# Last layer: POOL takes the subtractions that split queries and keys into bf16 parts

## The reference

```python
def _L3_attn_ref(x, Wq, Wk, Wv, Wo):      # N_HEADS 16, head width 8, sequence 256
    q = shape_heads(x @ Wq.T)
    k = shape_heads(x @ Wk.T)
    v = shape_heads(x @ Wv.T)
    q = q * cos + _rotate_every_two(q) * sin
    k = k * cos + _rotate_every_two(k) * sin
    scores = jnp.einsum('bhqd,bhkd->bhqk', q, k) * scale
    scores = scores + mask[None, None]
    attn = jax.nn.softmax(scores.astype(jnp.float32), axis=-1).astype(q.dtype)
    out = jnp.einsum('bhqk,bhkd->bhqd', attn, v)
    ...
    return out @ Wo.T
```

## Time and profile before

| | |
|---|---|
| time, median of 3 runs | 768.75 us (766.16 to 769.16) |
| profiled execution, its own time | 766.3 us |
| span of the profiled execution | 765.0 us |
| busy: PE, PEld, DVE, ACT, POOL | 720.3, 572.4, 499.3, 441.5, 252.3 us |
| mean granted TensorE clock, share of full speed | 0.972 |

### The profile page before, as it was taken

The page is one execution under the profiler, slowest core; times in us unless marked ns, Lnnn a source line. Parts: engine busy times, 40 slices in busy tenths (PEclk is TensorE's granted clock), DMA queues, the critical chain, the costliest instruction groups (busy, mean ns, idle before and its releaser), DMA issues.

```text
span 765.0 us, 14977 instructions
## 1 busy us (share of the span) xinstructions
PE 720.3 (94%) x5760; PEld 572.4 (75%) x5760; DVE 499.3 (65%) x1321; ACT 441.5 (58%) x944; POOL 252.3 (33%) x267
## 2 busy tenths in 40 slices
PE   7799999999999889999999999999979799999996
PEld 4577886678787667877779998698768467767764
DVE  1656788548967766668763757476548477776652
ACT  4526788458885785686635655235421465554664
POOL 1375355562515722233670126851003500000000
PEclk8869999999999999999999999999999899999999
DMA  9811453425311140000026664568885404207000
GB/s 298 251 54 45 138 163 95 138 84 165 88 50 46 34 153 1 1 1 2 29 86 202 200 191 146 185 197 253 261 219 125 90 16 117 58 2 160 17 17 15
DMA packets 71221, 84.00 MB, mean 110 GB/s; under 512 B 7199, under 2 KB 55914, under 8 KB 71146
## 3 DMA queue, kind: packets, MB, share of 16 engines
q1 hardware_dynamic: 67054, 74.65, 33.7%
q0 software_dynamic: 4096, 8.40, 3.6%
HBM read 65.46 MB, written 17.43 MB: 108 GB/s over the span
## 4 chain that ended last, share of the span: by engine, by line
PE 77%; DVE 6%; DMA 5%; ACT 5%; POOL 4%; issue 2%; SPq 1%; POOLq 0%; ACTq 0%; DVEq 0%
PE bank L929 5%; PE bank L938 4%; PE bank L861 4%; PE bank L849 3%; PE bank L674 3%; PE bank L536 3%; PE bank L495 3%; PE bank L720 3%; PE bank L496 2%; PE bank L697 2%; PE bank L807 2%; PE bank L893 2%; PE bank L789 2%; PE bank L590 2%; PE bank L666 2%
## 5 line engine op out<-in xcount | busy, mean ns | idle before, releaser
L1970 DVE TENSOR_REDUCE arena<-bank 128x2 f32<-128x512 f32 (+1 forms) x96 | 63.7, 684 | 20.7 <-PE bank L763 11.1
L1285 ACT ACTIVATE arena<-bank 128x512 f32<-128x512 f32 x96 | 55.9, 597 | 35.7 <-PE bank L791 27.8
L495 PE MATMUL bank<-ones 128*128 128x256 bf16 x275 | 69.1, 282 | 2.9 <-POOL ones L2277 1.7
L496 PE MATMUL bank<-ones 128*128 128x256 bf16 x275 | 69.0, 281 | 0.0
L929 PE MATMUL bank<-room 128*128 128x128 f32 x368 | 49.1, 277 | 1.6 <-DMA room<-in_wx 1.6
L938 PE MATMUL bank<-room,h 128*128 128x128 f32 x368 | 49.2, 277 | 0.0
L929 PEld LDWEIGHTS bank<-room 128*128 128x128 f32 x368 | 44.8, 192 | 3.3 <-DMA room<-in_wx 1.9
L938 PEld LDWEIGHTS bank<-room,h 128*128 128x128 f32 x368 | 45.1, 192 | 2.2 <-issue 1.9
L2254 POOL DMA_INDIRECT sent<-own,arena x32 | 32.8, 1024 | 30.2 <-DVE arena L1646 21.3
L2170 POOL TENSOR_SCALAR rs<-mv 128x4 f32<-128x4 f32 x20 | 6.5, 327 | 106.7 <-DVE mv L1466 84.9
L2254 POOL DMA_INDIRECT sent<-own,room x32 | 36.1, 1128 | 14.2 <-issue 8.1
(11 more groups left out here) (410 smaller groups left out, 2082.5 us busy)
## 6 DMA issues: line engine op xcount, KB each, us to landing
room<-in_wx SPq DMA_DIRECT2D x46, 578.0 KB, 5.2
room<-in_wx SPq DMA_DIRECT2D x46, 257.0 KB, 3.2
answer<-room SPq DMA_DIRECT2D x44, 128.0 KB, 3.3
room<-sent SPq DMA_DIRECT2D x20, 256.0 KB, 3.4
W<-part SPq DMA_DIRECT2D x12, 384.0 KB
room<-part SPq DMA_DIRECT2D x12, 384.0 KB
sent<-acc SPq DMA_DIRECT2D x10, 256.0 KB, 4.2
part<-arena SPq DMA_DIRECT2D x12, 128.0 KB, 2.7
```

What stands on the lines that cost most here:

```text
L495: pe.matmul(banks[bank][:, 0:256], busy[:, 0:128], busy, start=True, stop=True)
L496: pe.matmul(banks[bank][:, 256:512], busy[:, 0:128], busy, start=True, stop=True)
L1285: act.activation(PT[n % 4], banks[(3, 6)[n % 2]][:], ACT.Exp).then_inc(*S.step("PT", tb, n))
L1970: dve.tensor_reduce(mx[:, tb % 2, bb, int(k < 2), h:h + nh], banks[1 + n % 2][:].rearrange("p (h t) -> p h t", h=nh), AX.X, ALU.max).then_ ...
```

## The change

The two subtractions per `w` leave DVE's `heads3` and go into POOL's, behind `prep` (the norm) of the same block. The arithmetic is the same. ACT's waits for `rest` now look at POOL. In ORDER sixteen steps "A" leave the vector string, from the block of the last layer on, and sixteen join the pool string.

```diff
@@ scalar, heads3
-                    S.wait_ge(*V.end("rest", tb, w, 0))
+                    S.wait_ge(*G.end("rest", tb, w, 0))
                     act.copy(dst(1), rres).then_inc(*S.step("mid", tb, w))
                     yield
-                    S.wait_ge(*V.end("rest", tb, w, 1))
+                    S.wait_ge(*G.end("rest", tb, w, 1))
                     act.copy(dst(2), rres).then_inc(*S.step("part", tb, w))
@@ vector
-            def split3(tb, w):
-                src, tmp, dst = rr[0], rres, lambda n: parts[:, w, n, :]
-                V.wait_ge(*S.end("high", tb, w))
-                dve.tensor_tensor(tmp, src, dst(0), ALU.subtract).then_inc(*V.step("rest", tb, w, 0))
-                yield
-                V.wait_ge(*S.end("mid", tb, w))
-                dve.tensor_tensor(tmp, tmp, dst(1), ALU.subtract).then_inc(*V.step("rest", tb, w, 1))
-                yield
...
                     dve.tensor_tensor(rr[0], rr[0], rr[1], ALU.add).then_inc(*V.step("roped", tb, w))
                     yield
-                    yield from split3(tb, w)
                     t = S.end("part", tb, w)
@@ pool, heads3
                 yield from prep(l, tb)
+                for w in range(2):
+                    G.wait_ge(*S.end("high", tb, w))
+                    pool.tensor_tensor(rres, rr[0], parts[:, w, 0, :], ALU.subtract).then_inc(*G.step("rest", tb, w, 0))
+                    yield
+                    G.wait_ge(*S.end("mid", tb, w))
+                    pool.tensor_tensor(rres, rres, parts[:, w, 1, :], ALU.subtract).then_inc(*G.step("rest", tb, w, 1))
+                    yield
@@ ORDER, pool, the last line
-        "A1 C6 A1 C5 R1 C3 B1 C1 B1 A4 C1 A3 C5 A2 C12 A7"),
+        "A1 C6 A1 C5 R1 C3 B1 C1 B1 A8 C1 A7 C5 A2 C12 A15"),
```

## The result

The changed kernel took 770.67 us, the median of nine runs (768.99 to 776.47), against 767.37 us for the kernel before in the same session (763.63 to 770.75). The ratio is 1.0076, 95% interval 1.0053 to 1.0100: slower by 4 to 7.7 us. The plain difference of the two medians is smaller, 3.3 us, and that of the means is 4.2, so the size of the loss is known to a microsecond or two. The forecast was 5.1 us, 0.66%. The profiled execution took 770.75 us. All ratios here leave out executions more than 1.5% above the fastest of their own kernel (none of these eighteen).

What follows compares the result with a forecast made beforehand. The prediction took PE's own instruction list as the likely bound. Its terms, 0.6 + 0.1 + 3.1 + 1.3 = 5.1 us, on 768.75 gave 773.85, say 773.8 us (0.66% slower); range 769.4 to 777.2, with 0.51 on the forecast.

Steps and rivals of the forecast that it cites:

- Block 2, keys, +3.1: DVE's add slides behind the second reduction; ACT's cast holds up an exponent; PE stalls 3.1 us at L812 (2.9 to 3.4).
- The clock, +1.3: Behind the stall at L812, PE runs at about half clock for a while: 1.3 us more, bounds 0 and 1.7.
- The rival that it holds: The stall at L812 comes but the clock stays full: 772.6 us, chance 0.22.
- POOL's subtraction, 1.26 us: Each 128x512 subtraction takes 1.26 us on POOL, between 1.04 and 1.46, so 0.57 more than on DVE.
- the rival of a POOL slowed to 1.7 us: Every POOL subtraction meets a two-operand DVE operation and takes 1.7 us: 775.6 us in all, chance 0.10.
- Block 0, queries, +0.6: Third cast 0.9 us later, so the parts' transfers move; part comes out at the first peaks: 0.6 us, bounds 0 and 0.9.
- Block 0, keys, 0: Later third cast hidden by 2.5 us before SP's issue; PE up to 1.6 us late, absorbed by the 4.47 us stall.
- Block 1, 0: Keys' add slides behind two reductions, yet the activation PE wants is in time by 0.8 us: no cost.
- Blocks 2 (queries) and 3: Block 2's queries: ACT's waits absorb most of 0.9 us, +0.1; block 3: ACT's exponents outlast the longer subtractions, 0.
- DVE's relief, 0: DVE's 11 us less work gains nothing; the rival that it counts had 764.6 us, chance 0.05.

Runs made afterwards that it cites:

- the run with the add kept: Changed kernel with all sixteen subtractions on POOL, but DVE's add of roped (L1951) back in its place in every block: ratio 1.0022 (768.55 us).
- the late add on DVE: Kernel before, subtractions still on DVE; block 2's keys' add and two subtractions put behind both reductions: 1.0020 on the second chip, 1.0056 (816.69 us) on the third.

## Why the prediction was right, and where it wasn't

**Block 2, keys, +3.1: right, and the main cause.** Predicted 639.75 for L812 from a reduction at 637.24; in the trace 639.81 from 637.27, a wait of 3.05 us, with ACT idle for 4.87 ahead of the cast. It comes with the late add whoever subtracts, goes with the add's return, and goes (in part to another instruction) when ACT's order lets the exponent pass.

**The clock, +1.3: right.** The rival that it holds is out: 0.55 behind the stall, 1.00 when the stall is filled, and 1.15 to 1.65 us between L812 and the next L775.

**POOL's subtraction, 1.26 us: too long by 0.11.** It took 1.154 to 1.156 us by the medians of its two lines, and no neighbour stretched one in this trace; the longest in any run was 1.25. So the rival of a POOL slowed to 1.7 us is out. ACT waited 1.26 us for each, which the prediction took as 1.34. The estimate by the Trainium skill's figure (GPSIMD Engine Reference, 3.1), 1.12 us, lies 0.03 below what was measured, nearer than the middle of the bounds.

The rival's mechanism is real, but found no occasion in this kernel: none of its subtractions runs beside a DVE TENSOR_TENSOR of operands in SBUF. In three of the four kernels on POOL whose add kept its place in block 2, one does, as the recurrence's step then runs beside it. DVE, then POOL, in the run with the add kept:

```profile
636.34 0.42 DVE L2114 TENSOR_TENSOR wa<-wa 128x256 f32<-128x256 f32 x1
636.79 1.13 DVE L2116 TENSOR_SCALAR yT<-wa 128x256 f32<-128x256 f32 x1
...
636.53 1.24 POOL L2230 TENSOR_TENSOR arena<-arena 128x512 f32<-128x512 f32 x1 [5.53 <-ACT arena L1265]
```

The subtraction took 0.09 us more, and DVE's next, which takes 0.29 as a rule, took 1.13 and ended 0.15 behind the subtraction. The rows are the same to 0.01 us in the other two. There the trace agrees with the Trainium skill's rule on DVE and GpSimd shutting each other out (SBUF — State Buffer, Who interferes with whom). It cost PE nothing: from L812 to the next L775 it took 4.66 us, as before. The prediction looked for the price on POOL's side, and DVE paid it.

**Block 0, queries, +0.6: the start of the mechanism right, the size open.** ACT's casts of block 0, beside the earlier trace rows:

```profile
527.19 0.62 ACT L1265 CAST arena<-arena 128x512 bf16<-128x512 f32 x1 [3.15 <-DVE arena L1951]
529.07 0.62 ACT L1268 CAST arena<-arena 128x512 bf16<-128x512 f32 x1 [1.26 <-POOL arena L2230]
530.96 0.62 ACT L1271 CAST arena<-arena 128x512 bf16<-128x512 f32 x1 [1.27 <-POOL arena L2233]
```

From the first cast to the third it is 3.77 us against 3.02: 0.75 later, not 0.9. The issue of the keys' parts stands 16.28 us behind the first cast in both kernels (546.71 - 530.43, 543.47 - 527.19), so SP made up for it as predicted. The first peaks were forecast 0.6 us late and came 0.31 late by the same measure. (They were forecast at 569.2 and came at 565.70, as the whole layer began 3.24 earlier.)

Over all profiles the transfer seems to land later. From the issue of the keys' parts to the read-back behind it, the trace before has 8.8 us (the 8.78 of the earlier trace rows). SP's rows of the changed kernel, of the run with the add kept, and of the late add on DVE:

```profile
543.47 0.43 SPq L2387 DMA_DIRECT2D part<-arena  x1
...
552.46 1.36 SPq L2409 DMA_DIRECT2D W<-part  x3
```

```profile
542.31 0.43 SPq L2387 DMA_DIRECT2D part<-arena  x1
...
552.63 1.28 SPq L2409 DMA_DIRECT2D W<-part  x3
```

```profile
586.37 0.43 SPq L2390 DMA_DIRECT2D part<-arena  x1
...
595.16 1.29 SPq L2412 DMA_DIRECT2D W<-part  x3
```

It is 8.61 to 9.26 us in the five with DVE's subtractions (mean 8.91), 8.99 to 10.62 in the eight with POOL's, done once (mean 10.06; the changed kernel itself has the 8.99), and 11.03 with each done twice. So 0.75 us of lateness of the queries' parts goes with 1.15 us on the mean at the keys' read-back, above the bound of 0.9. That a late transfer meets more traffic in these queues would explain it, and is not shown. How much of it reaches the peaks isn't settled either, since from the read-back's issue to the peaks it took 13 to 17 us in the one kind and 13 to 18 in the other. The two POOL kernels without block 2's late add stand 0.9 us above the kernel before, plus or minus 1.3 (means of 24 and 35 runs), and the changed one 4.2 plus or minus 2.9 above the late add on DVE on the third chip. A cost of POOL of 1 to 2 us fits both; that it is nothing on the first chip, or more on the slower ones, where the changed kernel is 8.7 us above the kernel before, is possible too. No run here settles the term.

**Block 0, keys, 0: right.** The third cast ended 13.22 us behind the first one's start, 3.1 us ahead of the issue of the parts (2.5 were forecast). PE was 0.8 us late at L938, within the 1.6 allowed, and the stall ahead of the peaks took it in.

**Block 1, 0: right.** Counted from the first peaks, the keys' first cast was forecast 2.87 us behind them and came 2.88 behind (568.58 - 565.70), and PE's L938 behind it (572.13) waits for nothing. POOL's fetches of answers started at 581.46, 9.15 us behind its last subtraction of block 1, when the answers had landed, so its new work held up none of them. **Blocks 2 (queries) and 3:** behind 610 the shift between the traces moves by 0.2 us at most outside the stall and its half clock. PE's wait for the transfer behind block 3's heads (L789) is 0.3 us in the kernel before and none to 0.7 in the five with POOL's on chips of that speed.

**DVE's relief, 0: right.** DVE has 10 us less to do, and no kernel with the subtractions on POOL was measured faster than its counterpart with them on DVE.

**The sum.** 3.05 for the wait and 1.35 for the clock make 4.4 us, which the rows show one by one. What POOL's length adds lies between nothing and 2 us. The total of 4.4 to 6.4 fits the 4 to 7.7 of the ratio, and the 3.3 and 4.2 of the medians and means if POOL adds little. The forecast's 5.1 had the two large terms right by their mechanism; that the small ones came out near enough was partly luck, as nothing here measures them. The time found, 770.67, lies 3.1 us below the 773.8 forecast. 1.4 of that is the base: three runs had 768.75 and nine have 767.37. The other 1.8 is the 5.1 us forecast against the 3.3 between the medians. The wait at L775 was 7.1 us here and 4.8 to 5.4 in the five other profiles of that chip's speed, one of which has the same lists on DVE and POOL. DVE waited there for a fetch of answers, so the longer wait belongs to that execution and not to the change.

## What to carry to other kernels

When steps are taken out of a hand-written order, look at what slides into their places: the moved work cost some 2 us at most on the first chip, and an untouched add that took the wrong slot cost 4.4. Follow the slid instruction through the in-order queue of the engine that waits for it, to the first thing that the bounding engine wants from behind it. A stall of the bounding engine (here PE, 3.05 us) cost its length and then the clock, 1.35 us more; and a stall that is filled by reordering is only gained if the next in each queue is ready too.

## What the runs showed that was not expected

The same program took 767 us on one chip and 809 to 811 us on two others, with the same durations of POOL's subtraction (1.152 to 1.156 us), and with waits of ACT that the profile puts down to no one. Of the 49 us between two profiled spans of the changed kernel (818.5 and 769.5), 42.5 are lost ahead of the last layer (its first cast starts at 569.72 and at 527.19); what loses them no run was made to show. Inside the last layer the waits on these chips are others too, and an experiment made for a wait of the first chip (L775) found it gone.

The other is the pair on DVE and POOL: a short DVE operation begun during one of POOL's took four times its length, 1.13 us for 0.29, and ended with it.
